# Probabilities times V in one run per pair of heads, and O^T drained in the same pair

## What is computed

```python
A1 = Q1 @ K1^T / sqrt(64);  A2 = Q2 @ K2^T / sqrt(64)
P  = softmax(A1) - lam * softmax(A2)
O  = P @ V                       # 512 x 64 for each head and sequence
Y  = concat(O) @ Wo + bo         # later layer-normalised, scaled by 0.2
```

## Time and profile before

| | us |
|---|---|
| median of 3 runs | 1941.71 |
| lowest, highest | 1940.66, 1942.69 |
| the profiled execution, its own time | 1935.32 |
| its span in the trace | 1933.5 |

### The profile page before, as it was taken

How to read it: one execution, slowest core, us unless ns; L and a number is a source line. 1 busy time by engine, 2 the same in 40 slices (tenths; PEclk the granted TensorE clock), 3 DMA queues, 4 the chain that set the end, 5 groups by cost and what they waited for, 6 DMA issues and landing times. The chain is left out here.

```text
span 1933.5 us, 33239 instructions
## 1 busy us (share of the span) xinstructions
PE 1856.4 (96%) x10753; PEld 1442.1 (75%) x10753; DVE 1512.5 (78%) x2500; ACT 1417.2 (73%) x3298; POOL 703.8 (36%) x757
## 2 busy tenths in 40 slices
PE   5999999999999999999999999999999499999997
PEld 4866777777777777777777777777776399999896
DVE  5588888888888888888888888888888376666265
ACT  5588888888888888888888888888888376666100
POOL 2144333333333333333322333322223375555443
PEclk9799999999999999999999999999999799999999
DMA  8689888888888888888898888888885666666898
GB/s 290 181 219 258 212 221 224 225 223 234 225 222 225 225 228 228 207 231 227 220 232 230 225 222 227 222 228 227 220 212 137 241 208 238 234 236 212 285 385 285
DMA packets 228132, 446.09 MB, mean 231 GB/s; under 512 B 28962, under 2 KB 119888, under 8 KB 221968
## 3 DMA queue, kind: packets, MB, share of 16 engines
q1 hardware_dynamic: 223216, 434.02, 81.5%
q0 software_dynamic: 4768, 10.25, 1.8%
HBM read 184.34 MB, written 58.50 MB: 126 GB/s over the span
## 5 line engine op out<-in xcount | busy, mean ns | idle before, releaser
L536 ACT ACTIVATE e<-p_score,nmax 128x512 f32<-128x512 f32 x1024 | 695.4, 685 | 149.1 <-DVE nmax L743 145.5
L743 DVE TENSOR_REDUCE nmax<-p_score 128x2 f32<-128x1024 f32 x512 | 621.8, 1214 | 209.2 <-PE p_score L850 205.3
L386 POOL TENSOR_SCALAR e<-e,rrec,lam 128x512 f32<-128x512 f32 x512 | 394.6, 771 | 971.0 <-DVE rrec L708 971.0
L850 PE MATMUL p_score<-ks,qs 128*128 128x512 f32 x2048 | 580.3, 405 | 3.4 <-ACT e L536 3.3
L850 PEld LDWEIGHTS p_score<-ks,qs 128*128 128x128 f32 x2048 | 366.2, 189 | 177.6 <-issue 101.7
L815 PE MATMUL p_proj<-xh,w 128*128 128x512 f32 x1024 | 386.6, 418 | 5.8 <-POOL xl L370 3.7
L715 DVE SCALAR_TENSOR_TENSOR pm<-e,rrec 128x512 f32<-128x512 f32 x512 | 385.3, 753 | 0.7 <-POOL e L386 0.7
L470 ACT COPY pT<-p_tr 128x512 f32<-128x512 f32 x512 | 301.1, 588 | 96.8 <-PE p_tr L860 89.1
L860 PEld LDWEIGHTS p_tr<-consts,pm 128*128 128x128 f32 x2048 | 248.9, 140 | 88.5 <-issue 27.4
L860 PE MATMUL p_tr<-consts,pm 128*128 128x128 f32 x2048 | 308.5, 273 | 4.3 <-ACT pT L470 4.3
L875 PE MATMUL p_pv<-pT,v 128*64 128x512 f32 x1024 | 247.7, 605 | 2.0 <-DVE oT L720 2.0
(11 more groups left out here) (141 smaller groups left out, 1895.8 us busy)
## 6 DMA issues: line engine op xcount, KB each, us to landing
ks<-k_parts SPq DMA_DIRECT2D x512, 256.0 KB, 4.4
qs<-q_parts SPq DMA_DIRECT2D x512, 128.0 KB, 2.7
w<-weight_parts_scratch SPq DMA_DIRECT2D x56, 1024.0 KB, 9.3
w<-in_w SPq DMA_DIRECT2D x46, 1024.0 KB, 7.2
oT_scratch<-oT SPq DMA_DIRECT2D x64, 512.0 KB
op<-oT_scratch SPq DMA_DIRECT2D x32, 1024.0 KB
wv<-weight_parts_scratch SPq DMA_DIRECT2D x56, 256.0 KB, 7.9
weight_parts_scratch<-w SPq DMA_DIRECT2D x8, 1024.0 KB
```

Source lines behind the costliest of these rows:

```text
L386: nc.gpsimd.tensor_scalar(e2, e2, rrec[:, g % 4, 1:2], lam[:, 0:1], ALU.mult, ALU.mult).then_inc(s_e2, 1)
L536: nc.scalar.activation(ex[:, g % EX, m, :], p_score[g % 2][:, m, :], ACT.Exp, bias=nmax[:, g % 2, m:m + 1], accum_out=rsum[:, g % 4, m:m + ...
L743: vec.tensor_reduce(nmax[:, g % 2, :], p_score[g % 2][:, :, :], AXX, ALU.max, negate=True).then_inc(s_max, 1)
L850: last_op = nc.tensor.matmul(p_score[g % 2][:, m, :], qs[j][u][:, m, qt * P:(qt + 1) * P], ks[j][u][:, m, part, :], start=(part == 0), sto ...
```

## The change

The four key tiles of O^T of the pair before are all multiplied in step 5 (`PV_STEP = 5`), and none in step 7. ScalarE's copy of O^T and VectorE's low part are both taken in step 7 of the pair in which the products run (`O_STEP = 7`) instead of in steps 0 and 1 of the next. After the loop only the last pair's copy and low part are left. The calls of `store_o` stay where they are.

```diff
--- before.py
+++ after.py
@@ -188,7 +188,7 @@
         ORDER = ("q0", "k0", "q1", "k1")
         AT_STEP = {0: "q0", 1: "k0", 2: "q1", 3: "k1"}
         V_STEP = 6
-        PV_STEP = {5: (0, 1), 7: (2, 3)}
+        PV_STEP, O_STEP = 5, 7
 
         def batch_of(pair):
             return pair // PAIRS
@@ -518,8 +518,8 @@
 
             for g in range(STEPS):
                 pair, st = g // TPP, g % TPP
-                if st == 0 and pair >= 2:
-                    copy_o(pair - 2)
+                if st == O_STEP and pair >= 1:
+                    copy_o(pair - 1)
                 what = AT_STEP.get(st - 1)
                 if what and pair + 1 < NPAIRS:
                     high_part(pair + 1, what)
@@ -550,7 +550,6 @@
                         high_qk(pair + 3, 1)
             for g in range(STEPS - LAG, STEPS):
                 copy_pT(g)
-            copy_o(NPAIRS - 2)
             copy_o(NPAIRS - 1)
 
         @block.vector
@@ -751,8 +750,8 @@
                     add_bv(g - FIRST_V)
                 if st == 0 and 1 <= pair <= NPAIRS - 2:
                     add_bv(2 + pair - 1)
-                if st == 1 and pair >= 2:
-                    low_o(pair - 2)
+                if st == O_STEP and pair >= 1:
+                    low_o(pair - 1)
                 for _ in range(ROUTE_OPS[g] if g < len(ROUTE_OPS) else 0):
                     next(route_on)
             assert next(route_on, "over") == "over"
@@ -760,7 +759,6 @@
                 reciprocals(g)
             combine(STEPS - 2)
             combine(STEPS - 1)
-            low_o(NPAIRS - 2)
             low_o(NPAIRS - 1)
 
         @block.tensor
@@ -860,22 +858,20 @@
                     last_op = nc.tensor.transpose(p_tr[:, k, :], pm[:, g % 4, k * P:(k + 1) * P], ident)
                 last_op.then_inc(s_tr, 1)
 
-            def times_v(pair, key_tiles):
+            def times_v(pair):
                 j, it = pair % 2, pair // 2
-                if key_tiles[0] == 0:
-                    pe.wait_ge(s_pT, (pair + 1) * TPP)
-                    pe.wait_ge(s_v, 2 * it + 2)
-                    if pair == 0:
-                        pe.wait_ge(s_rd, ONEHOT + 3)
-                    if pair >= 1:
-                        pe.wait_ge(s_olo, pair)
-                for k in key_tiles:
+                pe.wait_ge(s_pT, (pair + 1) * TPP)
+                pe.wait_ge(s_v, 2 * it + 2)
+                if pair == 0:
+                    pe.wait_ge(s_rd, ONEHOT + 3)
+                if pair >= 1:
+                    pe.wait_ge(s_olo, pair)
+                for k in range(QT):
                     for u in range(2):
                         c = j * P + u * D
                         last_op = nc.tensor.matmul(p_pv[u * D:(u + 1) * D, :], v[it % 2][:, k, c:c + D],
                                                    pT[j][u][:, k, :], start=(k == 0), stop=(k == QT - 1))
-                if key_tiles[-1] == QT - 1:
-                    last_op.then_inc(s_pv, 1)
+                last_op.then_inc(s_pv, 1)
 
             pe.wait_ge(s_const, 16)
             transpose_x(0)
@@ -905,8 +901,8 @@
                 scores(g)
                 if g >= LAG:
                     transposes(g - LAG)
-                if st in PV_STEP and pair >= 1:
-                    times_v(pair - 1, PV_STEP[st])
+                if st == PV_STEP and pair >= 1:
+                    times_v(pair - 1)
                 if g == RANK_STEP:
                     ranks()
                 if st in AT_STEP and pair + 1 < NPAIRS:
@@ -917,7 +913,7 @@
                     values(2 + pair, 4 * (pair + 1) + 4)
             for g in range(STEPS - LAG, STEPS):
                 transposes(g)
-            times_v(NPAIRS - 1, range(QT))
+            times_v(NPAIRS - 1)
 
 
 def ffn_and_output_stage(nc, ins, xn_d, token_d, ys_d, oT_d, consts, tile_expert, slot_u, prob, out):
```

## The result

The changed kernel takes 1960.38 us (median of 4 runs, 1957.51 to 1961.89) against 1941.18 for the kernel before: a ratio of 1.0097, with a 95% interval of 1.008 to 1.0115, or +19.2 us. Run again later it gave 1962.3 and 1.0104 (1.0082 to 1.0125). The forecast was 1958, slower.

The account below looks back on a forecast made before the run. TensorE was taken to set the pace; -0.33 + 0.81 - 0.19 = +0.29 us a pair over 61 pairs, +17.7, less 1.2 at the end, gave +16.5 and 1958 us. Forecast's own range 1946 to 1975; 80% range 1938 to 1974.

Parts of the forecast that it names:

- (a): TensorE's products all in step 5: step 5 grows 1.71 us, step 7 falls 2.04, TensorE's own work falls 0.33 a pair.
- (e): VectorE enters step 2 without its lag, shortening steps 4 and 5: gain 0.19 us a pair, bounds 0 and 0.26.
- (b): Scores of steps 0 and 1 after the longer step 5: no wait for exponentials, by 0.23 us in step 0.
- (c): Copy of O^T on ScalarE moved to step 7, fitting roughly into its wait: 0, bound 0 to 0.15 us a pair.
- (d): Low part moved to step 7: unbroken VectorE chain of 6.24 us against TensorE's 5.43, a 0.81 us wait in step 1.
- the end of the stage: Last pair but one's copy and low part no longer delay the last products: 1.2 us taken of a 1.98 wait.
- the first: Rival: the wait in step 1 does not come and the change is faster, 1909 us; chance 0.15.
- The second, by occupancy: Rival: no difference; if VectorE's total work set the pace, the time would stay 1941.7 us; chance 0.12.
- The third, the clock: Rival: TensorE's 61 waits each lower the granted clock, much slower, 2062 us; chance 0.04.

Follow-up runs that it names:

- the run alone: Changed kernel, but copy of O^T back in step 0 and its low part back in step 1 of the next pair: 1949.96 us, ratio 1.0047.
- the low part at step 1: Changed kernel, but only the low part of O^T back in step 1 of the next pair, copy still in step 7: 1936.36 us, ratio 0.9973.
- e8: Changed kernel, but in the last pair products in steps 5 and 7 and drain as in the kernel before: 1956.36 us, ratio 1.0098.
- e3: Changed kernel, but copy and low part of O^T both in step 6: 1929.9 us, ratio 0.9942.
- e5: Changed kernel, but copy and low part of O^T in step 6 and the V bias before the combination in step 0: 1920.56 us, ratio 0.9897.
- the low part twice: Changed kernel, but the low part of O^T computed twice in step 7, the second after the first has ended: 2006.05 us, ratio 1.0333.

## Why the prediction was right

*The path.* TensorE sets the pace in starts, and the change makes it wait for VectorE at one place. Where the whole chain is in the trace, it is without idle time, a second low part in it comes out in full, shortened by either of two links the wait nearly goes, and shortened by both it is gone.

*Term by term.* (a) Step 5 was to grow by 1.71 and step 7 to fall to 1.28: the run takes 3.58 and step 7 lasts 1.29. TensorE's own work and the lag of (e), -0.33 and -0.19 a pair in the forecast, are together -0.47 in the kernel without waits, where -0.52 was forecast. (b) No wait for the exponentials came in the pairs that have V's projection. In pair 62, which has none in step 6, it did: that pair is 1.5 longer, and I had counted it like the others. By the forecast's own figures this wait could have been seen: the exponentials take 3.96 us from the scores of step 6, and TensorE, without the projection, has only two short steps of work until then. Those two last 1.39 and 2.70 us in the changed kernel, 4.09 together. (c) The copy of O^T in step 7 costs nothing, and the bound above 0 wasn't needed. What the forecast did not see is that in step 0 it had become a cost as soon as the products run together (the run alone against the low part at step 1). (d) The chain was put at 6.24 us from the scores of step 7 and is 6.21 (845.19 to 851.40); the wait, put at 0.81, is 0.78. (e) The lag of VectorE in steps 3 and 4 is gone: step 4 is 1.28 in all pairs from the sixth on. The forecast's 0.13 and 0.26 for it are not sums of the rows that it names; measured from steps 4 and 5, with 1.72 us for the joined run, it is some 0.09 in odd and 0.22 in even pairs, 0.15 for the 0.19 taken. A pair: +0.29 forecast, +0.29 measured. That it fits to the hundredth is luck, since the wait was put 0.03 too high and the gain of (e) 0.04 too high; that it fits to a tenth is not.

*The mis-sized term* is the end of the stage: 1.2 us less were forecast from the wait of 1.98, and against the second trace of before the last stretch became 0.4 to 0.9 longer. The transposes behind the last step and the last run of products in the changed kernel, then that run in the second trace of before:

```profile
1520.22 0.63 PE L858 MATMUL p_tr<-consts,pm 128*128 128x128 f32 x4 [2.02 <-DVE pm L714]
1522.04 1.09 PE L858 MATMUL p_tr<-consts,pm 128*128 128x128 f32 x4 [1.20 <-ACT pT L470]
...
1527.51 5.84 PE L872 MATMUL p_pv<-pT,v 128*64 128x512 f32 x16 [0.68 <-ACT pT L470]
```

```profile
1510.34 6.58 PE L875 MATMUL p_pv<-pT,v 128*64 128x512 f32 x16 [1.98 <-DVE oT L720]
```

The wait did fall as forecast, from 1.98 to 0.68. But the run behind it starts 27.7 us after the last pair's first scores, and 26.0 before: the long run in step 5 puts off the last scores, and TensorE then waits 2.02 and 1.20 for VectorE and ScalarE. In e8, with the last pair as before, the run starts after 25.5 again (at the full clock throughout, the first trace of before has 25.4), so the loss belongs to the joined run in that pair, of which the forecast took only the gain. The end is 2.1 us above its forecast and pair 62 1.2; pairs 2 to 4 grew by 0.3 instead of three times 0.29. That makes the difference between the 16.5 us of the forecast and 19.2.

*The rivals.* The wait came, so the first falls, though moving one instruction of VectorE makes it true. The second, by occupancy, had VectorE's total as the bound and no change in time: e3 and e5 change no instruction's cost, only places, and move the time by 30 and 40 us against the changed kernel. The third, the clock, did not happen: the granted clock is 1.00 over pairs 5 to 61, even with a wait of 1.5 us in each (the window of the low part twice). The forecast's evidence for it, the full clock in the first 19 us of the last pair, holds in all 14 traces; behind it, 20.8 to 24.6 us after that pair's first scores, the clock fell in 13 of them.

## What to carry to other kernels

When two engines alternate, a step made short on the leading one takes away the slack of the other: before joining two runs of work, add up the follower's starts over the steps behind, up to the first wait that the leader has on it. A small operation then goes where the follower is idle (here step 6), and an operation that another engine waits for goes ahead of one that can wait. Starts and their distances gave this to 0.1 us a step; shares of busy time would not have. The regular stretch does not speak for the ends: where a pair lacks the work that fills its steps, the sum has to be made again.

## What the runs showed of the chip that I had not expected

The same kernel, traced twice, kept the clock at 1.00 in the last pair once (28.5 us) and had 0.84 the other time (32.0 us): of 14 traces of all kernels, 13 have the lower clock there. TensorE had waits of up to 2 us in that stretch in the trace that kept the clock, and in the other trace the same waits as that one (0.96, 0.23, 0.92 and 0.16 us ahead of its scores, 0.93 ahead of transposes) until the clock fell, 21.7 us after the first scores. So the waits don't tell the two apart, and the cause of the drop stays open. And the attention stage began between 65.3 and 71.3 us in these 14 traces, although no kernel differs ahead of it, so single traces of this kernel can't be compared by their spans; the stretches between the same two instructions, in pairs 5 to 61, repeat to 0.2 us (1268.08 and 1268.19, 1284.68 and 1284.69).
